# Attention and MoE layer on one core: the order of the row-maximum tiles and of the first scores of a unit is changed

## The reference

```python
q = (x @ Wq) -> 16 heads of 16;  k, v = x @ Wk, x @ Wv -> 4 heads of 16, each used by 4 query heads
att = q k^T / 4 + slope_h * (j - i), causal
y = softmax(att) v @ Wo
x1 = layernorm(x + y)
out = layernorm(x1 + shared_ffn(x1) + top-1 of 8 experts(x1))
```

## Time and profile before

| | us |
|---|---|
| median of 3 executions | 646.47 (646.07 to 650.15) |
| span of the profiled execution, first to last instruction | 642.6 |
| around the span (median less span) | 3.9 |
| attention, first scores of unit 0 to end of the last weigh | 71.5 to 335.1 |
| one unit in the middle | 33.1 |

### The profile page before, as it was taken

One profiled execution on the slowest core, in us unless ns is written; L12 is line 12 of the kernel. 1 busy time (PEld: TensorE's weight loads), 2 busy tenths in 40 slices (PEclk: granted clock), 3 DMA queues, 4 the chain that ended last, 5 costly groups with the idle time before them and its releaser, 6 DMA issues.

```text
span 642.6 us, 8817 instructions
## 1 busy us (share of the span) xinstructions
PE 558.7 (87%) x2602; PEld 262.7 (41%) x2603; DVE 305.3 (48%) x630; ACT 214.2 (33%) x311; POOL 127.6 (20%) x186
## 2 busy tenths in 40 slices
PE   5957799999999999998597999999999888888870
PEld 2322333333333333332125665666655444544440
DVE  1459586868686868685007543222122322223221
ACT  1320255555565555565460021110122122211210
POOL 3511000000000000000001006830024443444433
PEclk9967699999999999999888699999999999999996
DMA  6498303112120313191962700220222111121111
GB/s 224 130 237 227 65 18 62 38 47 53 39 59 31 50 36 61 24 337 22 338 170 82 259 0 2 102 95 0 68 73 60 55 58 56 50 56 50 41 41 24
DMA packets 41327, 55.29 MB, mean 86 GB/s; under 512 B 5703, under 2 KB 29513, under 8 KB 41266
## 3 DMA queue, kind: packets, MB, share of 16 engines
q1 hardware_dynamic: 29490, 31.47, 18.5%
q10 hardware_dynamic: 8836, 15.36, 7.6%
q0 software_dynamic: 2976, 8.14, 4.1%
HBM read 36.26 MB, written 18.50 MB: 85 GB/s over the span
## 4 chain that ended last, share of the span: by engine, by line
PE 49%; DMA 14%; DVE 13%; issue 10%; POOL 6%; SPq 2%; ACT 2%; ACTq 1%; POOLq 1%; DVEq 0%
DMA out<-rows,tokj 9%; DVE mx L856 9%; PE ps L476 9%; PE ps L602 9%; PE ps L500 9%; PE ps L489 6%; PE ps L613 4%; PE ps L488 2%; PE ps L574 2%; DMA qk_or_dn<-mrow 2%; PE ps L444 2%; POOL zrs L1135 2%; POOL rows L1128 2%; DVE rows L1047 1%; SPq L296 1%
## 5 line engine op out<-in xcount | busy, mean ns | idle before, releaser
L856 DVE TENSOR_REDUCE mx<-ps 128x1 f32<-128x512 f32 (+4 forms) x312 | 186.4, 645 | 56.4 <-PE ps L478 42.2
L783 ACT ACTIVATE probs<-ps 128x1024 f32<-128x1024 f32 x144 | 140.4, 1021 | 115.8 <-PE ps L489 108.8
L476 PE MATMUL ps<-qk_or_dn 103*128 103x512 bf16 (+3 forms) x384 | 115.8, 344 | 17.4 <-DMA qk_or_dn<-qparts 7.1
L489 PE MATMUL ps<-qk_or_dn 103*128 103x512 bf16 x288 | 93.3, 391 | 6.9 <-ACT probs L783 6.7
L680 PE MATMUL ps<-wgu,tmp 128*128 x184 | 84.7, 603 | 4.9 <-issue 4.8
L476 PEld LDWEIGHTS ps<-qk_or_dn 103*128 103x128 bf16 x384 | 37.3, 99 | 124.8 <-DVE mx L856 99.8
L500 PE MATMUL ps<-probs,Vs 128*32 128x512 f32 x576 | 77.9, 613 | 1.3 <-ACT probs L783 1.2
L1047 DVE TENSOR_SCALAR rows<-rows,zmv,zrs 128x256 f32<-128x256 f32 x23 | 9.5, 414 | 101.2 <-POOL zrs L1135 101.2
L478 PE MATMUL ps<-cb 128*128 128x128 bf16 x256 | 52.7, 230 | 0.0
L680 PEld LDWEIGHTS ps<-wgu,tmp 128*128 128x128 f32 x184 | 33.1, 189 | 42.6 <-issue 42.5
L829 ACT ACTIVATE tmp<-ps 128x512 f32<-128x512 f32 x23 | 13.7, 597 | 93.6 <-PE ps L691 93.6
(11 more groups left out here) (110 smaller groups left out, 485.7 us busy)
## 6 DMA issues: line engine op xcount, KB each, us to landing
wgu<-in_gu ACTq DMA_DIRECT2D x8, 1024.0 KB, 6.2
qk_or_dn<-qparts SPq DMA_DIRECT2D x48, 128.0 KB
yT<-yU SPq DMA_DIRECT2D x16, 256.0 KB, 2.1
qk_or_dn<-in_dn SPq DMA_DIRECT2D x8, 512.0 KB, 8.2
qparts<-tmp SPq DMA_DIRECT2D x8, 384.0 KB, 3.1
tmp<-xs SPq DMA_DIRECT2D x23, 128.5 KB, 2.1
tmp<-yT SPq DMA_DIRECT2D x34, 64.0 KB
xs<-rows ACTq DMA_DIRECT2D x1, 2056.0 KB
```

The source lines that it names most:

```text
L476: mm = pe.matmul(o, q, K6[k][0:KROWS, k0:k0 + w], start=True, stop=not masked)
L489: mm = pe.matmul(o, K6[k][0:KROWS, kb * P:(kb + 1) * P], Q6[k][0:KROWS, :, qi * P:(qi + 1) * P], start=kb != qi, stop=True)
L783: act.activation(probs[:, 4 * (s % 3) + 2 * hb:4 * (s % 3) + 2 * hb + 2, :], ps[:, 4 + 2 * hb:6 + 2 * hb, :], ACT.Exp, scale=SCALE).then_i ...
L856: dve.tensor_reduce(o, ps[:, a_bank(u, t), 0:nh * w].rearrange("p (h w) -> p h w", h=nh), AX.X, ALU.max).then_inc(s_amax, 1)
```

## The change

Three things are changed together.

- **One stream of tiles, spread evenly.** `max_stream(u)` is the order of the tiles on PE and DVE: unit u's tiles 0 and 1, then the transpose of unit u-1 (`LEAD = 2`), then tiles 2 to 38. Nine places of it (`AHEAD = 9`: tiles 0, 1, transpose, 2 to 7) go before the step in which they used to begin: at the end of the step before. `LOTS` gives each of nine groups 4 or 5 tiles in turn. Places are counted through by `max_index`, and a tile's bank is its place modulo 2, still two banks.
- **First scores ahead.** The group loop runs from 1 to 9, and the scores of group 0 of unit u+1 (`first_scores`, with the wait for `s_mrow`) come ahead of weigh 8 of unit u. ACT takes the exponentials of these scores ahead of its copy of the second half of y, and its weight loads and `zero_slots` now stand ahead of groups 1 to 5 (unit 6), 1 to 3 and 4 (unit 7).
- **No loop on PE and DVE.** All eight units are written out there; ACT, SP and POOL keep their loops.

```diff
-LOT = (1, 2, 2)
+LEAD, AHEAD = 2, 9
+LOTS = ((1, 1, 2), (2, 1, 2)) * 4 + ((1, 1, 2),)
+def max_index(u, t, last=False):
+    if t == NA - 1:
+        return u * NA + NA - 1 if last else (u + 1) * NA + LEAD - 1
+    if isinstance(u, int) and u == 0:
+        return t
+    return u * NA + (t - 1 if t < LEAD else t)
+def max_stream(u):
+    own = [(u, t) for t in range(NA - 1)]
+    if u == 0:
+        return own
+    return own[:LEAD] + [(u - 1, NA - 1)] + own[LEAD:] + ([(u, NA - 1)] if u == NU - 1 else [])
...
-                sp.wait_ge(s_amax, u * NA + NA)
+                sp.wait_ge(s_amax, max_index(u, NA - 1, last) + 1)
...
-                    pe.wait_ge(s_amax, u * NA + t - 1)
+                    pe.wait_ge(s_amax, max_index(u, t, u == NU - 1) - 1)
...
+            def first_scores(u):
                 pe.wait_ge(s_mrow, u * 48 + 48)
                 pe.wait_ge(s_vs, u + 1)
+                for hb in range(2):
+                    scores(u, u % STEP, 0, hb)
...
+            def step(u):
+                k = u % STEP
+                todo = max_stream(u + 1)[AHEAD:] if u + 1 < NU else []
+                if u + 2 < NU:
+                    todo += max_stream(u + 2)[:AHEAD]
+                for s in range(1, GROUPS + 1):
+                    a, b, c = LOTS[s - 1]
+                    if s < GROUPS:
+                        scores(u, k, s, 0)
+                        some(todo, a)
+                        scores(u, k, s, 1)
+                        some(todo, b)
+                    else:
+                        some(todo, a + b)
+                        if u + 1 < NU:
+                            first_scores(u + 1)
+                    weigh(u, k, s - 1)
+                    some(todo, c)
...
-            max_tile(0, 0, NA - 1)
-            with pe.Fori(0, LOOPS, 1) as it:
...
+            some(max_stream(1)[:AHEAD], AHEAD)
+            first_scores(0)
+            for u in range(NU):
+                step(u)
...
+            def step(u, last=False):
+                for s in range(1, GROUPS):
+                    if isinstance(u, int) and u == NU - 2 and s <= 5:
+                        load_gate_up(s - 1)
+                    if last and s <= E - 5:
+                        load_gate_up(4 + s)
+                    if last and s == E - 4:
                         zero_slots()
+                    weights(u, s)
...
+                if not last:
+                    weights(u + 1, 0)
                 act.wait_ge(s_pv, u * GROUPS + GROUPS + 3)
                 act.wait_ge(s_yst[1], u * 16 + 16)
                 act.activation(yU[:, 1, :], ps[:, 3, :], ACT.Copy).then_inc(s_yev, 1)
...
+            split_max(0)
+            for u in range(1, NU):
+                for v, t in max_stream(u):
+                    if t == NA - 1:
+                        turned_max(v)
+                    else:
+                        reduce_tile(v, t)
+                        if t == NA - 2:
+                            split_max(v)
```

94 lines of the change are left out of this document (30 added, 64 removed).

## The result

| | kernel before | changed kernel |
|---|---|---|
| median, us | 648.31 (646.07 to 651.95, 4 runs) | 659.19 (658.29 to 659.98, 4 runs) |
| ratio, 95% interval | | 1.0163 (1.0126 to 1.0201) |
| span of the profiled execution | 642.6 | 657.9 |

The account below looks back on a forecast made before the run. PE was taken as the bound, though with gaps. Start -0.1, units 1 to 5 +2.5, unit 6 -0.1 and unit 7 +1.8 gave +4.1 on 642.6; with 3.9 more, 650.6 us against 646.47, range 641.5 to 654.

Parts of the forecast that it names:

- The unit term: First scores of one middle unit to the next: 33.6 us against 33.1, +0.5 each, +2.5 for units 1 to 5.
- the clock: Rival: PE's clock falls in longer idle ahead of first scores, 2.2 us a unit, 13 in all, 664 us; chance 0.05.
- behind attention: Stages from 335 us on: claimed to keep their cover, with no term in the sum.
- The rules by which I walked PE and DVE through a unit: Durations and start delays of tiles, reductions and scores, taken from unit 4's rows, to lay out the new order.
- The front: First scores to weigh 0 of a unit: 4.35 us instead of 4.87, saving 0.52.
- the seam: Tile 38 to the next unit's first scores: 7.1 us against 6.93 before.
- The wait for the row maxima: PE ahead of next first scores: not hidden but growing, idle about 1.4 us instead of 0.6.
- The 23 waits for two banks: PE's weight loads waiting for reductions, 12.3 us a unit: order alone leaves the gaps; rival that they vanish, chance 0.05.
- The middle from weigh 0 to tile 38: Within a unit: 22.19 us with one weigh more, against 21.30 before.
- The start: Up to unit 1's first scores: 106.7 instead of 106.76 us, -0.1, between -1.6 and +0.5.
- Unit 7: Last attention unit, set by ACT's queue of DMAs: +1.8 us, between -2.2 and +4.1; rival losing all 4.1, chance 0.10.
- The base: Profiled span of 642.6 us, with the median of the runs taken to lie 3.9 above it.

Follow-up runs that it names:

- e10: The changed kernel with only the tiles' places altered: no pair between the halves of the scores in five-tile groups, pairs behind the scores and the weigh; 651.13 us, ratio 1.0094.
- e5: The changed kernel run again without any edit, in a later set; 658.68 us, ratio 1.0184 to the kernel before.
- b1: The kernel before, unedited, profiled again on one chip with the changed kernel; 649.09 us, ratio 1.0012.
- b2: The changed kernel, unedited, profiled again on one chip with the kernel before; 657.03 us, ratio 1.0120.
- e9: The kernel before, unedited, run and profiled again in a later set; 642.40 us, ratio 0.9984.
- e6: The changed kernel with 40 small unread fills put into DVE's program ahead of its first reduction; 658.00 us, ratio 1.0169 to the kernel before.
- e1: The kernel before with PE's and DVE's units written out, order unchanged; 644.80 us, ratio 1.0016.

## Why the prediction was wrong

Two steps of the sum failed that the runs can price. The unit term was mis-sized, +2.5 us for units 1 to 5 where 3.75 were measured. And the clock, which I gave nothing in the sum and a chance of 0.05, costs 1.6 us in the mean, since it falls behind some of the very waits that I had forecast. The mechanism of the units was right. These two do not carry the whole of the miss. Much of what is left lies behind attention, where I had nothing, and its cause is open.

**What held.** The rules by which I walked PE and DVE through a unit came out within 0.04 us a group: forecast 3.98, 3.33, 3.83, 3.11, 3.43, 3.23, measured 4.02, 3.36, 3.86, 3.15, 3.47, 3.26. The front is 4.36 (forecast 4.35), the seam 7.06 (7.1), the copy 0.46 behind the transpose (0.45). The wait for the row maxima grew as said, and to the size of 1.05 with 0.26 ahead of the transpose, where I had 1.4 and 0.4. The exponential of unit 7 is held on ACT's queue, for group 4. That a pair between the halves of the scores is the worse place is shown by e10, 0.63 us a unit. The 23 waits for two banks stayed, as many as before; that an order alone leaves such gaps holds for this order only, since e10 has 19 with the same two banks.

**The unit term was mis-sized.** +0.5 was forecast and +0.75 measured. The middle from weigh 0 to tile 38 is 22.41 where I had 22.19, six groups with 0.03 to 0.04 too little each; the rest is rounding. Five units made 1.25 us of it, a third of my whole sum.

**The clock was priced in the wrong shape.** I set it aside as all units or none, 2.2 us each and 13 in sum, chance 0.05, "against: with 0.6 idle the clock stands at 1.00". It comes or not at each wait: 7 of 42, 1.6 us each. With six such waits that is 1.6 us in the mean, and in the profile it is most of unit 6, forecast -0.1 and measured +1.8 (33.09 in e5, without it: +0.2).

**The start** was forecast -0.1 and came out +1.3 at the first scores of unit 1, outside my own -1.6 to +0.5. I let the clock rise at the same moment as before, in front of weigh 0; it was still low in weigh 0. From there to the first scores of unit 1 it took 30.47 instead of 29.3, where unit 4, at full clock, took 29.47. But this is not shown to be the order's: in b1 the kernel before has its first scores of unit 1 at 108.26, in b2, on the same chip, the changed kernel at 107.92, and in both the clock is up only at 80. With the rise at the same moment the term is what I forecast, near nothing; the +1.3 compare it with a first trace in which the clock was up at 77.0. The first scores of unit 0 themselves came at +0.2, not +0.7.

**Unit 7** was forecast +1.8 and is +0.9 in three profiles (30.92, 30.91, 30.90), inside its bounds, all at a granted clock of 0.83 like the 30.04 before; at the 0.88 and 0.89 of e9 and e6 the two orders take 28.84 and 29.94. ACT's first load comes 2.3 behind the first scores (314.31), not 2.9, and the block of DMAs ends 3.4 later against them, not 4.05.

**The base.** I put 3.9 us around the span, the median less the profiled span. In each later profile it is 1.8, the profiled execution's own time less its span (659.65 less 657.9). By this the first profiled execution took about 644.4, quicker than the three whose median I used. It shifts no ratio, but 2.1 us of the 650.6 were made of it.

**And behind attention** I had nothing ("the stages from 335 us on keep their cover"), and 7.5 of the 15.3 us between the two spans lie there. 2.8 of them are the stand, which is the chip's; 1.7 are a half clock of PE in the shared network, 1.6 the lower clock of the stage behind unit 7, a form that the kernel before has too (41.46 in e9), and 1.5 lie in the experts, mostly POOL's wait, which e1 has in the old order. None of the last three is shown to be the order's or shown not to be. What I did miss is the late store of unit 6: it costs nothing in the first profile, but 0.4, 2.0 and 0.3 us in e5, e6 and b2.

In sum the steps of the change that are shown are 3.75 + 0.2 + 0.9 = 4.85 us, 6.45 with the clock behind the waits (1.6), and 7.15 with the late store (0.7 in the mean of the first profile, e5, e6 and b2), against 4.1 forecast. The medians of three sets say 10.9, 12.3 and 9.2. Of the 2.1 to 5.2 us in between, the half clocks of the network (1.7, 1.7 and 3.4 us in the three profiles of the changed kernel, none in the three of the kernel before), the lower clock behind unit 7, the longer experts (by 1.5 to 2.6 us in the same three) and the start may each be a part. Against it works that the kernel before has in two of its three profiles (e9, b1) a wait of 2.2 us for mrow ahead of the first scores of unit 2, which the changed kernel has in none. This is open.
